# A transformer layer in fp32 on one core: the queue of loads and the places of small statistics are rearranged in its last stage

## The reference

```python
x = L0_attn_hidden_states                       # (4, 512, 1024) float32
x = x + attn(layernorm(x), Wq, Wkv, Wo)         # 32 heads of 32, one shared key and value head,
                                                # ALiBi bias, causal softmax, then @ Wo
x = x + ffn(layernorm(x), qweight, weight_scale, weight_zero_point, bias)
# ffn: w = (unpack 6-bit codes of qweight - zero_point) * scale ; einsum('bsk,nk->bsn', x, w) + bias
```

## Time and profile before

| what | value |
|---|---|
| median of three runs | 876.34 us (871.62 to 879.45) |
| the profiled execution | 877.17 us, span 875.4 us |
| PE busy | 830.7 us (95% of the span) |
| DVE, ACT, POOL busy | 574.2, 380.0, 429.1 us (66, 43, 49%) |
| DMA, mean over the span | 144 GB/s |
| mean granted clock of PE | 0.974 |

### The profile page before, as it was taken

One profiled execution on the slowest core, in us unless ns is written; L12 is line 12 of the kernel. 1 busy time (PEld: TensorE's weight loads), 2 busy tenths in 40 slices (PEclk: granted clock), 3 DMA queues, 4 the chain that ended last, 5 costly groups with the idle time before them and its releaser, 6 DMA issues. The chain is left out here.

```text
span 875.4 us, 13638 instructions
## 1 busy us (share of the span) xinstructions
PE 830.7 (95%) x4616; PEld 598.3 (68%) x4616; DVE 574.2 (66%) x1582; ACT 380.0 (43%) x731; POOL 429.1 (49%) x320
## 2 busy tenths in 40 slices
PE   7999999979999999999999999997989799999987
PEld 4787878868655556555555555676878588878765
DVE  4866564656678788878878882235419547684677
ACT  3756345311467776776666664112311221040322
POOL 0000000000378888888788885363646267262455
PEclk8999999999799999999999999998999899999999
DMA  9767676593545556565566614542073503500012
GB/s 332 270 192 214 227 238 217 171 234 114 147 124 137 142 143 148 139 151 120 141 168 162 147 60 140 169 130 85 0 245 140 192 18 105 183 8 1 37 60 97
DMA packets 71389, 125.84 MB, mean 144 GB/s; under 512 B 7460, under 2 KB 16708, under 8 KB 71240
## 3 DMA queue, kind: packets, MB, share of 16 engines
q1 hardware_dynamic: 71168, 124.71, 48.3%
q10 hardware_dynamic: 152, 0.27, 0.1%
HBM read 85.61 MB, written 38.94 MB: 142 GB/s over the span
## 5 line engine op out<-in xcount | busy, mean ns | idle before, releaser
L1342 DVE CUSTOM_DVE_ANT_0 spill<-p_s,mask 128x128 bf16<-128x128 f32 (+3 forms) x512 | 223.8, 482 | 57.0 <-PE p_s L806 54.7
L579 POOL TENSOR_SCALAR_AFFINE_SELECT pt<-pt 128x512 f32<-128x512 f32 x128 | 81.8, 651 | 279.7 <-ACT pt L1076 279.7
L1076 ACT ACTIVATE pt<-p_st 128x512 f32<-128x512 f32 (+1 forms) x352 | 178.8, 560 | 88.3 <-PE p_st L833 87.8
L806 PE MATMUL p_s<-kst,xt 98*128 98x128 f32 (+3 forms) x512 | 151.6, 335 | 4.7 <-DVE kst L1285 2.7
L833 PE MATMUL p_st<-xt,kst 100*128 100x512 f32 (+1 forms) x352 | 142.9, 411 | 4.0 <-ACT pt L1076 3.0
L806 PEld LDWEIGHTS p_s<-kst,xt 98*128 98x128 f32 x512 | 100.8, 198 | 18.1 <-DVE mx L1342 3.6
L586 POOL TENSOR_TENSOR pt<-pt 128x1536 f32<-128x1536 f32 x32 | 111.8, 3492 | 2.7
L833 PEld LDWEIGHTS p_st<-xt,kst 100*128 100x128 f32 x352 | 67.9, 194 | 40.1 <-DVE ml L1349 18.8
L844 PE MATMUL p_o<-pt,vst 128*32 128x512 f32 (+3 forms) x1024 | 89.7, 445 | 0.0
L592 POOL TENSOR_TENSOR pt<-pt 128x1024 f32<-128x1024 f32 x32 | 76.7, 2398 | 0.0
L752 PE MATMUL p_o<-xt,wqh 128*128 128x512 f32 x136 | 55.4, 407 | 0.9 <-DVE wql L1256 0.8
(11 more groups left out here) (191 smaller groups left out, 1639.2 us busy)
## 6 DMA issues: line engine op xcount, KB each, us to landing
xt<-qh_d SPq DMA_DIRECT2D x64, 256.0 KB
xs<-in_x_t_dram SPq DMA_DIRECT2D x32, 256.0 KB, 6.4
qh_d<-qh SPq DMA_DIRECT2D x32, 256.0 KB, 3.1
ql_d<-ql SPq DMA_DIRECT2D x32, 256.0 KB, 3.8
xt<-ql_d SPq DMA_DIRECT2D x32, 256.0 KB
o_d<-o_st SPq DMA_DIRECT2D x32, 256.0 KB, 2.3
inv_b<-inv_d SPq DMA_DIRECT2D x32, 256.0 KB
ob<-o_d SPq DMA_DIRECT2D x32, 256.0 KB, 4.8
```

The lines of the kernel that those rows point to most:

```text
L579: pool.affine_select(out=own, in_=own, compare_op=ALU.is_ge, fill=0.0, base=0, pattern=[[0, 4], [1, P]], channel_multiplier=-1).then_inc(c ...
L806: pe.matmul(scores_of(n), qst[s % 4][0:R_MAX, j, qb * P:(qb + 1) * P], kst[0:R_MAX, b * S:b * S + keys], start=True, stop=True).then_inc(s ...
L1076: act.activation(pt[s % 2][:, j:j + heads, PT_AT[kb]:PT_AT[kb] + KB_LEN[kb]], p_st[:, place(k) % 3, 0:heads * KB_LEN[kb]].rearrange("p (j ...
L1342: dve.tensor_tensor_reduce(spill[:, SPILL_AT[qb]:SPILL_AT[qb] + keys], scores_of(n), mask[:, S - keys:S], 1.0, LOWEST, ALU.add, ALU.max, m ...
```

## The change

Six things change. The first scores wait for the first batch's keys (`k_done` 2), and the wait for all keys moves to the first transposed scores. `o_normal(5)` moves from attention step 29 to step 30. In the last step SP issues the loads of o blocks 8 to 11 and the reciprocals 8 and 9 ahead of the store of step 30, and the reciprocals of blocks 10 to 15 come by two transfers `load_inv_1` of four blocks each (blocks 8 and 9 are in the first once more) into a new buffer `inv_1` behind the last totals. The first half of the next x is loaded between the sixth and the seventh store of batches 0 and 1. The last batch has six slots for centred tiles (the three of `xc`, two of `inv_b`, one of `ob`). And `over_features` is called at other tiles: y-sum at o tile 4 instead of 2, mean at f tile 6 instead of 3 (1 instead of 2 for the last batch), the last y-sum at f tile 7 instead of 5 and the last squares at f tile 1 instead of 2; DVE's `rstd2`, `pair_low` and `offset` move with them, and POOL's `y_low` and `add_square` of the last batch are put in another order.

The diff is cut: the declarations, the copies of an edit on other engines (POOL, ACT and DVE take `xc_at`, `inv_at` and `inv_landed` in place of the fixed slots) and the stores of batch 1, which change as those of batch 0 do, are left out.

```diff
@@ -166,6 +166,8 @@
         with ExitStack() as early:
             o_b = tensors(early)("o_b", [P, CK, 2, S], F32R)
         wi = sb("wi", [P, CK, CK, P], F32R)
+        with ExitStack() as early:
+            inv_1 = tensors(early)("inv_1", [P, CK, S])
         yl = sb("yl", [P, CK, S], F32R)
         xc = sb("xc", [P, 3, S])
 
...
@@ -309,6 +315,23 @@
 
         def x2_part(t, m):
             return x2[t % 2][:, m, :]
+
+        def inv_turn(k):
+
+            return k if k < CK + 2 else k - (CK - 2)
+
+        def inv_at(k):
+            return inv_1[:, k - CK, :] if CK + 2 <= k < 2 * CK else inv_b[:, inv_turn(k) % 2, :]
+
+        def inv_landed(k):
+            if CK + 2 <= k < 2 * CK:
+                return inv_1_in[(k - CK) // 4], 16
+            return inv_in[inv_turn(k) % 2], 16 * (inv_turn(k) // 2) + 16
+
+        def xc_at(t, m):
+            k = CK * t + m
+            return xc[:, k % 3, :] if t < B - 1 else (xc[:, 0, :], xc[:, 1, :], xc[:, 2, :], inv_b[:, 0, :], inv_b[:, 1, :],
+                                                      ob[:, 3, :])[m % 6]
 
         def squares_of(t):
             return ysn[:, :] if t < B - 1 else ob[:, 2, :]
@@ -447,18 +470,17 @@
                     load_inv(7)
                     load_x2(0, 0)
                     load_x2(0, 1)
+                if s == STEPS - 1:
+                    for k in range(CK, CK + 4):
+                        load_o(k)
+                    load_inv(CK)
+                    load_inv(CK + 1)
                 if s > 0:
                     store_o(s - 1)
                 b = s // GROUPS - 1
                 if s % GROUPS == 6 and b >= 0:
                     sp.wait_ge(inv_done, 16 * b + 16)
                     sp.dma_start(inv_d[b, :, :], sums[:, :]).then_inc(inv_out, 16)
-                if s == STEPS - 1:
-                    for k in range(CK, CK + 4):
-                        load_o(k)
-                    load_inv(CK)
-                    load_inv(CK + 1)
-
 
             def load_x2(t, half):
                 at_least(sp, stored[t % 2][half], 64 * (t // 2))
@@ -481,9 +503,16 @@
             def load_inv(k):
                 b, g = k // CK, k % CK
                 sp.wait_ge(inv_out, 16 * (b + 1))
-                at_least(sp, o_norm, k - 1)
+
+                at_least(sp, o_norm, CK + 1 + k - 2 * CK if 2 * CK <= k < 2 * CK + 2 else k - 1)
                 src = inv_d[b].rearrange("(j r) q -> j r q", j=4)[:, g:g + 1, :].to_broadcast([4, 32, S])
-                sp.dma_start(inv_b[:, k % 2, :], src).then_inc(inv_in[k % 2], 16)
+                sp.dma_start(inv_at(k), src).then_inc(inv_landed(k)[0], 16)
+
+            def load_inv_1(half):
+                sp.wait_ge(pv_done, STEPS)
+                src = inv_d[1].rearrange("(j r) q -> j r q", j=4)[:, 4 * half:4 * half + 4, :].rearrange(
+                    "j (a g) q -> j a (g q)", a=1).to_broadcast([4, 32, 4 * S])
+                sp.dma_start(flat(inv_1[:, 4 * half:4 * half + 4, :]), src).then_inc(inv_1_in[half], 16)
 
             def load_wi(m):
                 if m < CK - 1:
@@ -519,11 +548,11 @@
             for s in range(STEPS):
                 attend(s)
             store_o(STEPS - 1)
+            load_inv_1(0)
+            load_inv_1(1)
+            for k in range(CK + 4, 2 * CK):
+                load_o(k)
             load_x2(1, 0)
-            for k in range(CK + 2, 2 * CK):
-                load_inv(k)
-                if k < CK + 6:
-                    load_o(k + 2)
             load_x2(1, 1)
             sp.wait_ge(inv_done, 16 * B)
             sp.dma_start(inv_d[B - 1, :, :], sums[:, :]).then_inc(inv_out, 16)
@@ -546,9 +575,11 @@
             load_o(2 * CK + 7)
             load_inv(2 * CK + 6)
             load_inv(2 * CK + 7)
-            for m in range(CK):
+            for m in range(6):
                 store(0, m)
             load_x2(2, 0)
+            store(0, 6)
+            store(0, 7)
             load_x2(2, 1)
 
             for k in range(3 * CK, 3 * CK + 4):
...
@@ -691,11 +724,11 @@
                     for k in range(3 * CK + 4, 4 * CK):
                         o_normal(k)
                         o_low(k)
-            y_low(0)
-            y_low(1)
-            for m in range(1, CK):
-                if m + 1 < CK:
-                    y_low(m + 1)
+            for m in range(CK):
+                y_low(m)
+                if m in (2, 4, 6):
+                    add_square(LASTB, m // 2)
+            for m in range(4, CK):
                 add_square(LASTB, m)
             for m in range(CK):
                 add_offset(LASTB, m)
@@ -797,7 +830,7 @@
                     pe.wait_ge(mx_clear, 2)
                     pe.wait_ge(q_freed, CK * LASTB + 1)
                     pe.wait_ge(kst_ext, B)
-                    pe.wait_ge(k_done, 2 * B)
+                    pe.wait_ge(k_done, 2)
                 if n % 16 == 0:
                     pe.wait_ge(q_in[s % 4], 64 * (s // 4) + 64)
                 if qb != 1:
@@ -827,6 +860,8 @@
                 b = s // GROUPS
                 if k == 0:
                     pe.wait_ge(m_in[s % 2], 32 * (s // 2) + 32)
+                if s == 0 and k == 0:
+                    pe.wait_ge(k_done, 2 * B)
                 if s == 0 and k == 1:
                     pe.wait_ge(vst_done, B)
                 free_bank(s, place(k))
@@ -971,19 +1006,19 @@
                     out_tile(t, m)
                     if (t, m) == (1, 0):
                         over_features(0, MEAN)
-                    if m == 2:
+                    if m == 4:
                         over_features(t - 1, YSUM)
                     if m == 6:
                         over_features(t - 1, SQUARES)
                 for m in range(CK):
                     ffn_tile(t - 1, m)
-                    if m == (3 if t < LASTB else 2):
+                    if m == (6 if t < LASTB else 1):
                         over_features(t, MEAN)
-                    if (t, m) == (LASTB, 5):
+                    if (t, m) == (LASTB, 7):
                         over_features(LASTB, YSUM)
             for m in range(CK):
                 ffn_tile(LASTB, m)
-                if m == 2:
+                if m == 1:
                     over_features(LASTB, SQUARES)
 
         @block.scalar
...
@@ -1374,10 +1409,8 @@
                         o_normal((s - 20) // 2)
                     if i == 9 and s in (21, 23, 25, 27, 29):
                         o_low((s - 21) // 2)
-                    if (s, i) == (STEPS - 3, 13):
-                        o_normal(5)
                     if s == STEPS - 2 and i == 3:
-                        for k in (6, 7):
+                        for k in (5, 6, 7):
                             o_normal(k)
                         for k in (5, 6, 7):
                             o_low(k)
...
@@ -1406,19 +1439,26 @@
             def centre2(t, m):
                 k = CK * t + m
                 dve.wait_ge(summed, 3 * t + MEAN + 1)
-                if k >= 3:
+
+                if t == LASTB and m < 3:
+                    dve.wait_ge(sq_added, 7 * t)
+                elif t == LASTB and m < 6:
+                    dve.wait_ge(o_lo, CK * B)
+                elif t == LASTB:
+                    dve.wait_ge(sq_added, 7 * t + max(m - 6, 1))
+                elif k >= 3:
                     before = k - 3
                     dve.wait_ge(sq_added, 7 * (before // CK) + max(before % CK, 1))
                 else:
                     dve.wait_ge(o_out, 16 * STEPS)
                 if 0 < t and m < 3:
                     dve.wait_ge(res_done, CK * min(t, 2))
-                dve.tensor_tensor(xc[:, k % 3, :], x2_part(t, m), p_mean2, ALU.subtract).then_inc(centred, 1)
+                dve.tensor_tensor(xc_at(t, m), x2_part(t, m), p_mean2, ALU.subtract).then_inc(centred, 1)
 
             def y_low(t, m):
                 k = CK * t + m
                 dve.wait_ge(y_hi, k + 1)
-                dve.tensor_tensor(y_part(t, m, 1), xc[:, k % 3, :], y_part(t, m, 0), ALU.subtract).then_inc(y_lo, 1)
+                dve.tensor_tensor(y_part(t, m, 1), xc_at(t, m), y_part(t, m, 0), ALU.subtract).then_inc(y_lo, 1)
 
             def sum_centred(t):
 
@@ -1521,10 +1561,10 @@
                         chain(t - 1, m)
                     if m == 5:
                         pair_low(t - 1, SQUARES)
-
-                rstd2(t - 1, 0)
-                pair_low(t, MEAN)
-                rstd2(t - 1, 1)
+                    if m == 6:
+                        rstd2(t - 1, 0)
+                        rstd2(t - 1, 1)
+
                 if t == 1:
                     dve.wait_ge(rows_in, 16)
                     dve.scalar_tensor_tensor(out=zs[:, :], in0=scal[:, CK:2 * CK], scalar=-1.0, in1=scal[:, 0:CK],
@@ -1532,15 +1572,17 @@
                     dve.wait_ge(zs_done, 1)
                 sum_normal(t - 1)
                 offset(t - 1, 0)
+                pair_low(t, MEAN)
+                offset(t - 1, 1)
                 for m in range(CK):
```

(17 more changed lines are left out.)

12 lines of the change are left out of this document (6 added, 6 removed).

## The result

The changed kernel takes 869.42 us (median of 20 runs, 864.07 to 876.43) against 875.89 us (20 runs): a ratio of 0.993, 95% interval 0.9911 to 0.995, or 6 us less. The forecast was 860 us with a range of 848 to 869. The profiled execution took 865.46 us (span 863.7), 4.0 us under its own median; that of before (877.17 us) lay 1.3 us above the median of the 20. So the two traces differ by 11.7 us where the medians differ by 6.5, and what is read from one trace has to be held against that.

The account below looks back on a forecast made before the run. It took PE's long row of matmuls as the bound, with gaps costing idle time plus low clock. Terms 0 + 1.3 - 2.2 - 8.9 - 1.0 - 4.4 - 1.2 = -16.4 us; 877.17 - 16.4 - 0.8 = 860 us, range 848 to 869.

Parts of the forecast that it names:

- the reciprocals of batch 1 in two transfers: Behind attention: two 1 MB loads on four engines delay the first mean; +1.3 us, bounds 2 us either side.
- o_normal(5): Attention step 29: moving this DVE product to step 30 brings everything up to the end of attention 2.0 us sooner.
- Rival (c): Behind attention: the 2 MB hold everything up, a loss below 56 GB/s; 878 to 885 us, chance 0.05.
- First scores: Start of attention: scores start 2.7 us sooner, the wait behind them grows from 1.7 to 4.4 us; gain 0.
- the count of nine: PE's timeline before: nine rows with idle time ahead, 1.04 to 6.54 us, seven of them behind 518 us.
- Mean of batch 1: FFN tile 6 instead of 3: the 2.23 us gap goes, then PE waits 1.7 us for POOL's o_low; -2.2 us.
- x between the stores and y-sum: Output projection: earlier x and later y-sum close the 6.54 and 1.04 us gaps; -8.9 and -1.0 us.
- The last part: Last batch: gaps of 1.55 and 2.61 us and low clock go, a 1.5 us wait for squares comes; -4.4 us.
- The tail: Very end: DVE's last eviction should only trail PE, as the statistics are ready sooner; -1.2 us.
- Rival (a): Behind attention: the two transfers run wide, L946 follows its tile at 588.5; 848 us, chance 0.15.
- Rival (b): Last stage: new short waits bring the low clock back, 8 us return; 864 to 871 us, chance 0.2.
- Rival (d): Last stage: gains don't add, another chain is next at 696 and 841; 867 to 872 us, chance 0.1.

Follow-up runs that it names:

- the kernel with three buffers: Changed kernel with the last batch's centred tiles in three buffers instead of six places, and POOL's old order of y_low and add_square: 870.73 us, ratio 0.9951.
- the wide kernel: Changed kernel with each of the two reciprocal transfers of batch 1 cut into four of 32 partitions: 847.98 us, ratio 0.971.
- Eight narrow transfers: Changed kernel with batch 1's reciprocals in eight one-tile transfers of 256 KB, four engines each; SP waits for the first two before loading x: 865.09 us, ratio 0.9891.

## Why the prediction was wrong, point by point

**The failed step is the term "the reciprocals of batch 1 in two transfers", +1.3 us.** It took the 2.0 us of o_normal(5) as lost in it, so the transfers themselves stood at +3.3. Measured in place they cost 12 us (0.993 - 0.9796) and 10 us on the kernel before. The mechanism was the one named: four engines, 97 GB/s, x and o tiles behind them. Its size was off in two ways. (1) The step that failed in it is the landing of tile 12. The first transfer was to land 13.8 us after the issue and took 18.0; tile 12 was to come 25.3 us after it and came after 30.3. I used the rate of one small load in flight (97 GB/s) for a stretch in which the windows show 82 to 111, and at its start 16 busy engines moved only 208 GB/s. From issue to first mean I had 40.5 us and the profiled execution 46.1; the 5.0 us of tile 12 are nearly all of that difference. (2) I took one value for something that varies by 7 us between executions: 46.1, 46.9, 49.8 and 53.1 us, where tile 12 was multiplied 30.3, 31.1, 34.0 and 37.3 us after the issue. Against the 37.2 us of the kernel before that is 9 to 16 us more, and I had 3.3. The low clock, which I left as it was, is no part of the miss. It starts earlier (588.8 us, against 595.2 before), but PE waits there in any case: from the end of o_normal(15) to the first mean it is 7.5 us, and was 7.1. Behind the first mean it lasts 4.3 us (to 605.9), where it lasted 5.6 (to 602.0). The bound of 2 us to either side was too tight: it allowed for a rate, and not for what the rate does to everything queued behind. Rival (c) was right in kind, set its threshold at 56 GB/s and got a chance of 0.05; the term grew gradually well before that threshold. Its mark, a first mean beyond 605 us, was passed in two of the four executions.

**The other terms together** were -19.7 us (0, -2.0, -2.2, -9.9, -4.4, -1.2). The kernel that has them without the two transfers measured -18 us (-21.5 to -14.3). One by one:

- *First scores: 0.* Right in mechanism: one wait of 5.51 us (I had 4.4) for DVE's maxima, which wait for ACT's cast, which waits for the same DMA as in the earlier trace rows (the row below). The clock is 0.52 from 193 to 200 us, where it was 0.76 before. Measured +1.5 us (-0.6 to +3.6), not told from zero.

```profile
194.13 0.62 ACT L1080 CAST qh<-qt 128x512 fp32r<-128x512 f32 x1 [9.98 <-DMA ql_d<-ql]
```

- *o_normal(5): -2.0 us.* Measured -2.0 (-4.3 to +0.4). The wait at 520.50 is gone. The wait of 2.12 us at 531.68 for ACT is not new: it is the row below of the kernel before, one of those over 1.04 us that the count of nine leaves out (another is the 1.08 us at 591.16; and of the seven counted for the last stage, the one at 520.50 lies in attention). In the execution of before the clock was 0.50 from 534 to 537 us behind it, in that of the changed kernel it stayed at 1.00. That accounts for SP's first load behind attention going out 3.7 us sooner in the changed kernel's trace and not 2.0. It is no gain of the change: the kernel with three buffers runs the same code there and shows 0.50 again.

```profile
533.80 0.80 PE L833 MATMUL p_st<-xt,kst 100*128 100x512 f32 x1 [2.13 <-ACT pt L1076]
```

- *Mean of batch 1: -2.2 us.* The gap is gone, but what came next was not what I named. PE waits 1.69 us for its FFN bank at 664.23, which I had called free within half a us, and not for POOL's last low part, which ends at 680.9 us, 79.3 us behind the first mean as before. About the size came out, by another wait.
- *x between the stores and y-sum: -9.9 us.* No gap and full clock where 6.54 and 1.04 us had been. The 6.54 came from one execution; four other kernels that keep this wait show 7.69, 7.74, 7.92 and 8.63 us. x alone measured -8 us; x and the moved statistics together -15 us, where -9.9, -2.2 and a part of the last term were forecast.
- *The last part: -4.4 us.* The waits of 1.55 and 2.61 us are gone, and the new wait for the squares is 2.19 us where I had 1.5. It brought 3.4 us of low clock (0.66 in the window from 834), which I had not counted; the run with the squares one f tile later took both away. The six buffers, with POOL's order, gave 2 us or nothing.
- *The tail: -1.2 us.* PE ends at 859.4 us and DVE's last eviction starts at 859.56: it only trails PE, as forecast.

**Rival (a)** gave 848 us and a first mean at 588.5 for transfers that run wide. They did not, but the kernel in which they are made to measured 847.98 us with the first mean at 587.8 (its ratio of 0.971 is 851 us on the 876.34 of the forecast, so the same 848 is partly luck). The working of the chain was right; what was wrong was how far the narrow case lies from it. **Rival (b)** came in part: the clock fell behind the squares' wait, and not behind the 1.69 us at 664. **Rival (d)** did not come: the gains of the last stage added.

The Trainium skill's page "DMA: Bandwidth & Descriptors" ("Why a DMA increments its semaphore by 16 and not by 1") says that the number of engines is the largest up to 16 that divides the slowest dimension of both sides. The trace agrees: share 0.26 with four rows in front, 0.98 when 32 partitions are in front. The same page's section "Bandwidth" says that transfers of 1 MiB reach 75% of the peak, which it has from loads to 128 partitions that GpSimd issued. Here 1 MB, issued by SP, moved 82 to 111 GB/s over four engines, where 392 GB/s were seen from 585 to 587 us, so the hint does not hold for a source with four rows in front.

Put together from the runs, the parts are +1.5 for the first scores, -2.0 for o_normal(5), -15 for x and the statistics, -2 for the six buffers with POOL's order and +12 for the transfers: -5.5 us, where the change as a whole measured -6.1.

## What to carry to other kernels

Look at the DMA share while one transfer is alone in flight: 0.26 means four engines, and making it larger only makes a longer plug: here a load of 256 KB behind it landed after 28.3 us instead of 7.4. Cost such an edit by when the *next* load lands and not by the transfer's own time. Before anything is merged, cut it so that partitions, and not four source rows, are the slowest dimension. When a profile of one execution is compared with another's, first see how each stands to its own median, and count every gap and every stretch of low clock in both, since some differ between executions of the same code.

## What was not expected of the hardware

- Broadcasts from memory stay slow even over all engines: 209 GB/s at a share of 0.98 in the wide kernel, against 386 GB/s at 1.03 for the plain loads behind them (rows above). In the changed kernel the mixture at 559 to 561 us shows 208 GB/s at 0.99. What limits it was not tried.
- Eight narrow transfers keep SP at their issue for 13.52 us, eight of the wide kernel for 3.9 us; the narrow ones seem to fill the queue of their four engines. That was seen in one trace of the narrow ones and two of the wide, and not tested further.
- The wait of 2.1 us near 532 us stands in ten of the fourteen traces. In five of them, that of the kernel before among them, some 3 us at or near the lower clock followed it, in the other five, the changed kernel among them, none. The wait of 2.19 us at 834.80 was followed by 3.4 us. A wait's length alone did not tell which.
